# An expert stage on Trainium2: chunk ring of eight, and residual rows added by an accumulating scatter

## The reference, cut to what matters

```python
x = x + _L0_ffn_ref(_L0_cond_ref(x, ...), ...)      # conv, 4-bit weights, two low-rank terms
z = _L1_cond_ref(x, cond_128, ...)                  # per batch entry a 64x64 kernel

logits = zf @ gate_w.T + gate_b                     # 8 experts
selected = argmax(softmax(logits), axis=-1)
out = 0
for j in range(8):
    out += where(selected == j, zf @ expert_w[j].T + expert_b[j], 0)
x = x + out
```

## Time and profile before

| | us |
|---|---|
| median of 3 runs (1543.79 to 1545.86) | 1543.8 |
| the profiled execution: its own time | 1545.5 |
| its span | 1544.0 |
| TensorE busy | 1443.0 (93%) |
| VectorE busy | 1123.6 (73%) |
| ScalarE busy | 762.5 (49%) |
| GpSimd busy | 153.5 (10%) |
| `wlr` (L1019), 184 operations, mean 1219 ns | 212.9 |
| `whr` (L693), 184 operations, mean 1056 ns | 188.0 |
| `add_rows` (L1013), 23 operations, mean 1215 ns | 28.0 |

### The profile page before, as it was taken

How to read it: one execution, slowest core, us unless ns; L and a number is a source line. 1 busy time by engine, 2 the same in 40 slices (tenths; PEclk the granted TensorE clock), 3 DMA queues, 4 the chain that set the end, 5 groups by cost and what they waited for, 6 DMA issues and landing times.

```text
span 1544.0 us, 20802 instructions
## 1 busy us (share of the span) xinstructions
PE 1443.0 (93%) x6831; PEld 1173.4 (76%) x6831; DVE 1123.6 (73%) x1058; ACT 762.5 (49%) x845; POOL 153.5 (10%) x217
## 2 busy tenths in 40 slices
PE   6886899999999999999999999999989599999996
PEld 5676788888888888888888888888855477777774
DVE  3562787877888787788778778784234488888885
ACT  3461554454555445455554544551112166666763
POOL 0112200000000000000000000000011223343440
PEclk8898999999999999999999999999999599999998
DMA  5567565655665565565556546555646655877960
GB/s 161 195 206 275 209 222 221 263 217 192 256 241 199 213 262 217 192 257 221 211 220 261 215 188 264 226 212 189 235 163 231 216 144 141 304 206 235 317 181 6
DMA packets 104366, 331.30 MB, mean 215 GB/s; under 512 B 17361, under 2 KB 24921, under 8 KB 104249
## 3 DMA queue, kind: packets, MB, share of 16 engines
q1 hardware_dynamic: 80478, 258.22, 44.8%
q0 software_dynamic: 22512, 71.32, 15.0%
q10 hardware_dynamic: 1298, 0.68, 0.2%
HBM read 295.04 MB, written 46.14 MB: 221 GB/s over the span
## 4 chain that ended last, share of the span: by engine, by line
PE 84%; DVE 5%; DMA 3%; ACT 3%; issue 2%; ACTq 1%; POOL 0%; SPq 0%; DVEq 0%; POOLq 0%
PE pair L1045 25%; PE pair L1047 24%; PE pair L1046 24%; PE pair L1094 3%; PE pair L1189 2%; DVE wlr L1019 2%; DMA am<-am_dn 1%; PE pair L1246 1%; DMA batch_kernels<-aggs 1%; PE pair L1104 1%; ACT whr L693 1%; PE pair L1196 1%; DVE wf L761 1%; PE pair L1107 1%; PE pair L1204 1%
## 5 line engine op out<-in xcount | busy, mean ns | idle before, releaser
L761 DVE TENSOR_TENSOR wf<-wf,term 128x1024 f32<-128x1024 f32 x308 | 377.1, 1224 | 93.7 <-ACT term L554 74.9
L554 ACT ACTIVATE term<-codes 128x1024 f32<-128x1024 int32 x308 | 321.1, 1055 | 106.9 <-DVE wf L761 106.9
L1045 PE MATMUL pair<-wh,hh 128*128 128x512 f32 x704 | 275.2, 391 | 4.0 <-DVE acc L800 2.6
L1047 PE MATMUL pair<-wh,hl 128*128 128x512 f32 x704 | 274.7, 390 | 0.0
L1046 PE MATMUL pair<-wl,hh 128*128 128x512 f32 x704 | 274.6, 390 | 0.0
L1045 PE MATMUL pair<-ring,wh 128*128 128x512 f32 x656 | 255.5, 390 | 1.3 <-issue 1.3
L800 DVE TENSOR_TENSOR acc<-acc,pair 128x1024 f32<-128x1024 f32 x176 | 214.2, 1217 | 57.8 <-PE pair L1047 57.8
L1047 PE MATMUL pair<-ring,wl 128*128 128x512 f32 x656 | 255.2, 389 | 0.0
L1046 PE MATMUL pair<-ring,wh 128*128 128x512 f32 x656 | 255.2, 389 | 0.0
L1019 DVE TENSOR_TENSOR wlr<-wraw,whr 128x1024 fp32r<-128x1024 f32 x184 | 212.9, 1219 | 3.3 <-ACT whr L693 3.3
L582 ACT ACTIVATE wh<-wf 128x1024 fp32r<-128x1024 f32 x44 | 46.7, 1060 | 339.2 <-DVE wf L776 339.2
(11 more groups left out here) (162 smaller groups left out, 1398.9 us busy)
## 6 DMA issues: line engine op xcount, KB each, us to landing
ring<-x_parts SPq DMA_DIRECT2D x320, 512.0 KB, 7.4
wraw<-exp_w SPq DMA_DIRECT2D x64, 512.0 KB, 10.9
x_parts<-stage POOLq DMA_DIRECT2D x24, 512.0 KB, 8.3
xg<-exp_b POOLq DMA_DIRECT2D x23, 512.0 KB, 7.2
codes<-codes_up SPq DMA_DIRECT2D x22, 512.0 KB, 7.5
codes<-codes_dn SPq DMA_DIRECT2D x22, 512.0 KB, 6.1
am<-am_dn SPq DMA_DIRECT2D x22, 512.0 KB
acc<-x_nat POOLq DMA_DIRECT2D x16, 512.0 KB, 10.3
```

The costliest lines, as they stand in the source:

```text
L554: return nc.scalar.activation(out, codes[:, n % 2], ACT.Relu, scale=scale, bias=-scale * bend)
L761: nc.vector.tensor_tensor(whole(n), whole(n), term[:, e % 2], op).then_inc(term_added, 1)
L1045: mm(ps, ah, bh, start=first, stop=False)
L1047: return mm(ps, al, bh, start=False, stop=last)
```

## The change

The rings `whr` and `wlr` get eight slots, so ScalarE writes chunk kt of a tile once TensorE is done with chunk kt of the tile before. `rows_transposed` moves from after chunk 3 to after chunk 1; `z_high` and `z_low` of a tile now come after chunk 2 of its own conversion. `x_dram` is gone: SP stores the tiles of `acc` straight into `out`. `gather_x` and VectorE's `add_rows` are gone. Instead ScalarE copies a finished tile's sums from PSUM to `yg` (four buffers) in `rows_out`, after all eight chunks of the next tile; GpSimd adds the bias to `yg` by an accumulating DMA; and the scatter is an indirect DMA that adds `yg` to the rows of `out`. `zidx` has four entries, shared by gather and scatter, so a tile's gather now waits for the scatter of four tiles earlier.

```diff
@@ -100,7 +100,6 @@
         bd_dram = nc.dram_tensor("batch_kernels", (B, CH, CH), F32, kind="Internal").ap()
         x1_dram = nc.dram_tensor("x1_parts", (NC, KT, P, 2 * CHUNK), F32, kind="Internal").ap()
         z_dram = nc.dram_tensor("z_rows", (N, L), F32, kind="Internal").ap()
-        x_dram = nc.dram_tensor("x_rows", (N, L), F32, kind="Internal").ap()
 
         ident = sb(ctx, "ident", [P, P])
         ones = sb(ctx, "ones", [P, P])
@@ -184,13 +183,11 @@
         stages = (stage0, stage1, stage2, ring)
 
         moe = ExitStack()
-        whr = sb(moe, "whr", [P, 4, L], F32R)
-        wlr = sb(moe, "wlr", [P, 4, L], F32R)
+        whr = sb(moe, "whr", [P, KT, L], F32R)
+        wlr = sb(moe, "wlr", [P, KT, L], F32R)
         zth = sb(moe, "zth", [P, 2, KT, ST], F32R)
         ztl = sb(moe, "ztl", [P, 2, KT, ST], F32R)
-        xg = sb(moe, "xg", [P, 4, L])
         wraw = sb(moe, "wraw", [P, 2, KT, L])
-        zg = sb(moe, "zg", [P, 2, L])
         tri = sb(moe, "tri", [P, P])
         iota_i = sb(moe, "iota_i", [P, P], I32)
         iota_f = sb(moe, "iota_f", [P, P])
@@ -226,8 +223,9 @@
         loads = sb(moe, "loads", [P, 2, NSP], I32)
 
         through = sb(moe, "through", [P, E], I32)
-        zidx = sb(moe, "zidx", [P, 2], I32)
-        xidx = sb(moe, "xidx", [P, 4], I32)
+        zidx = sb(moe, "zidx", [P, 4], I32)
+        yg = sb(moe, "yg", [P, 4, L])
+        zg = sb(moe, "zg", [P, 2, L])
         moe.close()
 
         pair = [ctx.enter_context(nc.psum_tensor(f"pair{i}", [P, 1024], F32)) for i in range(4)]
@@ -262,10 +260,9 @@
         x_stored = [sem(f"x_stored{i}") for i in range(2)]
         iotas, route_const, route_dve, route_mm, row_ready, slot_mm, table_ready, tiles_ready = (sem(n) for n in (
             "iotas", "route_const", "route_dve", "route_mm", "row_ready", "slot_mm", "table_ready", "tiles_ready"))
-        zidx_ready, xidx_ready = sem("zidx_ready"), sem("xidx_ready")
+        zidx_ready = sem("zidx_ready")
         zg_in = [sem(f"zg_in{i}") for i in range(2)]
-        xg_in = [sem(f"xg_in{i}") for i in range(4)]
-        xb_in = [sem(f"xb_in{i}") for i in range(4)]
+        yb_in = [sem(f"yb_in{i}") for i in range(4)]
 
         wraw_in = [[sem(f"wraw_in{b}{i}") for i in range(KT)] for b in range(2)]
         whr_ready, wlr_ready, chunk_mm = sem("whr_ready"), sem("wlr_ready"), sem("chunk_mm")
@@ -380,7 +377,7 @@
 
             for t in range(TILES):
                 sp.wait_ge(acc_added, TILES * (UNITS - 1) + t + 1)
-                sp.dma_start(x_dram[t * P:(t + 1) * P], acc[:, t]).then_inc(x_stored[t % 2], 16)
+                sp.dma_start(out[t * P:(t + 1) * P], acc[:, t]).then_inc(x_stored[t % 2], 16)
             sp.wait_ge(bdg_zero, 1)
             sp.dma_start(gts[:], gate_t).then_inc(gts_in, 16)
             for i in rounds(sp, TILES // 2):
@@ -467,59 +464,47 @@
                 pool.wait_ge(z_stored[k], 16 * TILES // 2)
                 pool.wait_ge(x_stored[k], 16 * TILES // 2)
 
-            def gather_z(i, s):
-
+            def gather(i, s):
+
+                wait(pool, out_done[s % 4], i * 16 + 16 * (s // 4))
                 wait(pool, tr_mm, i * 4 + s - 1)
                 pool.sem_inc(pool_passed, 1)
-                nc.gpsimd.tensor_copy(zidx[:, s % 2:s % 2 + 1], table[:, bass.ds(i * 4 + s, 1)]).then_inc(zidx_ready, 1)
+                nc.gpsimd.tensor_copy(zidx[:, s % 4:s % 4 + 1], table[:, bass.ds(i * 4 + s, 1)]).then_inc(zidx_ready, 1)
                 wait(pool, zidx_ready, i * 4 + s + 1)
                 pool.sem_inc(pool_passed, 1)
-                pool.indirect_dma_start(zg[:, s % 2], None, z_dram, bass.IndirectOffsetOnAxis(zidx[:, s % 2:s % 2 + 1], 0),
+                pool.indirect_dma_start(zg[:, s % 2], None, z_dram, bass.IndirectOffsetOnAxis(zidx[:, s % 4:s % 4 + 1], 0),
                                         bounds_check=last_row, oob_is_err=False).then_inc(zg_in[s % 2], 16)
-
-            def gather_x(i, s):
-
-                wait(pool, out_done[s % 4], i * 16 + 16 * (s // 4))
-                pool.sem_inc(pool_passed, 1)
-                nc.gpsimd.tensor_copy(xidx[:, s % 4:s % 4 + 1], table[:, bass.ds(i * 4 + s, 1)]).then_inc(xidx_ready, 1)
-                wait(pool, xidx_ready, i * 4 + s + 1)
-                pool.sem_inc(pool_passed, 1)
-                pool.indirect_dma_start(xg[:, s % 4], None, x_dram, bass.IndirectOffsetOnAxis(xidx[:, s % 4:s % 4 + 1], 0),
-                                        bounds_check=last_row, oob_is_err=False).then_inc(xg_in[s % 4], 16)
 
             def add_bias(i, s):
                 e = pool.value_load(eti[0:1, bass.ds(i * 4 + s, 1)], min_val=0, max_val=E - 1)
-                wait(pool, xg_in[s % 4], i * 16 + 16 * (s // 4 + 1))
-                pool.sem_inc(pool_passed, 1)
-                pool.dma_start(xg[:, s % 4], exp_b[bass.ds(e, 1)].broadcast_to([P, L]), accum_op=ALU.add
-                               ).then_inc(xb_in[s % 4], 16)
-
-            def scatter(i, s):
                 wait(pool, y_ready, i * 4 + s + 1)
                 pool.sem_inc(pool_passed, 1)
-                pool.indirect_dma_start(out, bass.IndirectOffsetOnAxis(xidx[:, s % 4:s % 4 + 1], 0), xg[:, s % 4], None,
-                                        bounds_check=last_row, oob_is_err=False).then_inc(out_done[s % 4], 16)
+                pool.dma_start(yg[:, s % 4], exp_b[bass.ds(e, 1)].broadcast_to([P, L]), accum_op=ALU.add
+                               ).then_inc(yb_in[s % 4], 16)
+
+            def scatter(i, s):
+
+                wait(pool, yb_in[s % 4], i * 16 + 16 * (s // 4 + 1))
+                pool.sem_inc(pool_passed, 1)
+                pool.indirect_dma_start(out, bass.IndirectOffsetOnAxis(zidx[:, s % 4:s % 4 + 1], 0), yg[:, s % 4], None,
+                                        bounds_check=last_row, oob_is_err=False, compute_op=ALU.add).then_inc(out_done[s % 4], 16)
 
             def tile(i, s):
                 left = NS if not isinstance(i, int) else NS - 4 * i - s
                 if left > 2:
-                    gather_z(i, s + 2)
-                    add_bias(i, s + 2)
-                scatter(i, s)
-                if left > 3:
-                    gather_x(i, s + 3)
-
-            gather_z(0, 0)
-            gather_z(0, 1)
-            for s in range(3):
-                gather_x(0, s)
-            add_bias(0, 0)
-            add_bias(0, 1)
+                    gather(i, s + 2)
+                add_bias(i, s)
+                if not (isinstance(i, int) and i == s == 0):
+                    scatter(*((i, s - 1) if s else (i - 1, 3)))
+
+            gather(0, 0)
+            gather(0, 1)
             for i in rounds(pool, NS // 4):
                 for s in range(4):
                     tile(i, s)
             for s in range(NS % 4):
                 tile(NS // 4, s)
+            scatter(NS // 4, NS % 4 - 1)
             for k in range(4):
                 pool.wait_ge(out_done[k], 16 * len(range(k, NS, 4)))
 
@@ -689,21 +674,29 @@
                 for kt in range(KT):
                     for b in range(2):
                         act.wait_ge(wraw_in[b][kt], load[b])
-                    wait(act, chunk_mm, i * 32 + KT * s + kt - 3)
-                    nc.scalar.activation(whr[:, kt % 4], wraw[:, bass.ds(buf, 1), kt].rearrange("p a n -> p (a n)"),
+
+                    wait(act, chunk_mm, i * 32 + KT * (s - 1) + kt + 1)
+                    nc.scalar.activation(whr[:, kt], wraw[:, bass.ds(buf, 1), kt].rearrange("p a n -> p (a n)"),
                                          ACT.Copy).then_inc(whr_ready, 1)
-                    if kt == 5 and not (isinstance(i, int) and 4 * i + s == NS - 1):
-                        z_high(i, s + 1)
+                    if kt == 2:
+                        z_high(i, s)
+                if not (isinstance(i, int) and i == s == 0):
+                    rows_out(*((i, s - 1) if s else (i - 1, 3)))
+
+            def rows_out(i, s):
+                act.wait_ge(chunk_mm, i * 32 + KT * (s + 1))
+                wait(act, out_done[s % 4], i * 16 + 16 * (s // 4))
+                nc.scalar.activation(yg[:, s % 4], pair[s % 2][:], ACT.Copy).then_inc(y_ready, 1)
 
             for k in range(2):
                 act.wait_ge(x_stored[k], 16 * TILES // 2)
             act.wait_ge(tiles_ready, TABLES)
-            z_high(0, 0)
             for i in rounds(act, NS // 4):
                 for s in range(4):
                     convert_high(i, s)
             for s in range(NS % 4):
                 convert_high(NS // 4, s)
+            rows_out(NS // 4, NS % 4 - 1)
 
         @block.vector
         def _(dve):
@@ -1007,34 +1000,22 @@
                 nc.vector.tensor_tensor(ztl[:, s % 2], pair[2 + s % 2][:].rearrange("p (k s) -> p k s", k=KT), zth[:, s % 2],
                                         ALU.subtract).then_inc(ztl_ready, 1)
 
-            def add_rows(i, s):
-                wait(dve, chunk_mm, i * 32 + KT * (s + 1))
```

(24 more changed lines are left out.)

## The result

The changed kernel takes 1588.2 us (median of 4 runs, 1584.2 to 1596.5) against 1543.8: ratio 1.029, 95% interval 1.0267 to 1.0312. It is slower by 44 us.

What follows compares the result with a forecast made beforehand. TensorE, busy 93%, was taken as the bound, with GpSimd's ring late next. Terms -3.8 - 3.8 + 25.0 - 2.2 + 4.5 + 4 = +23.7 us on 1543.8 gave 1567 us; own range 1552 to 1586, over rivals 1522 to 1592.

Steps and rivals of the forecast that it cites:

- the third rival: Accumulating scatter pays a full landing of its own: quiet chain 18.3 us, total +53.5, 1597 us; chance 0.12.
- Conversion: Weight chunks on VectorE and ScalarE: eight slots remove 0.95 us per tile, 22 intervals, 20.9 us if nothing else is late.
- The quiet ring: Products through bias, scatter, index copy and gather to transposes, without loads: 16.1 us; ten intervals at 12.7 against 13.08, -3.8.
- the last four: Last four tile intervals, whose gathers fetch nothing as routing fills 20 of 23 tiles: 12.13 us each, -3.8.
- bytes follow in the same queue: Scatter's bytes come after the bias's in one queue: 3.0 us added, bounds 0 (full overlap) and 5.2 (full landing).
- Beside the loads: Chain under weight loads: 25.1 us, two tiles 34.4 (+8.2) in long stretches, 30.5 (+4.3) in short; together +25.0.
- the four pairs: Two-tile rounds in the four weight-load stretches: two at +8.2 us, two at +4.3.
- Clock: TensorE at half rate after long pauses: 1.8 us lost in each of two pairs, +4 with rounding.
- Start: TensorE's first product in the stage: three chunks converted by then, -2.2 us (-1.1 if the clock's rise doesn't move).
- End: Last products to last scatter: copy 1.1, bias 5.2, scatter at about 6.5 instead of 2.0, +4.5 us (bounds +3.5 and +8).
- the chain fits: Rival: transfers overlap, chain stays under 15.0 us also with loads, all 22 intervals at 12.13; -18.6, 1525 us; chance 0.27.
- Its sign: What would prove the scatter's full landing: bias landings in quiet above 7 us in the new profile.

Runs made afterwards that it cites:

- run 1: Changed kernel with two GpSimd calls swapped: scatter of tile s-1 issued before the bias addition of tile s; 1543.4 us, ratio 0.9979.
- run 2: Changed kernel, GpSimd's order kept, scatter given its own copy of the row numbers so the gather waits for no scatter; 1548.4 us, ratio 1.0007.
- run 7: Kernel before with only the rings of eight and the earlier transposes, plus the gather one tile earlier (s+3); 1514.8 us, ratio 0.982.
- run 8: Changed kernel with own scatter index and gather one tile earlier; bias now written plainly two tiles ahead, VectorE adds the sums; 1514.5 us, ratio 0.9791.
- run 3: Changed kernel without the weight transfers of experts 2 to 7, whose tiles use the weights of experts 0 and 1; 1559.2 us, ratio 1.0081.
- run 5: Kernel before with rings of eight chunks and earlier transposes alone; residual gather, bias and plain scatter as before; 1545.8 us, ratio 1.0012.
- run 4: Changed kernel with a scatter that writes instead of adding, so the residual is left out of the result; 1569.6 us, ratio 1.0145.
- run 10: Repeat in five rounds of the kernel before with rings of eight and the gather one tile earlier; 1514.4 us, ratio 0.9817.

## Why the prediction was right, and where its sum was off

The direction and the mechanism held: TensorE waits for gathered rows, held up by the ring from the sums through the bias, the scatter and the index copy to the next gather, and runs 1 and 2 show it. The size did not: +24 us were forecast and +44 measured. 1588 us lies inside the range over all rivals (1522 to 1592), but 2 us above the forecast's own (1552 to 1586), and nearer the third rival's 1597 than the 1567. Its terms:

- **Conversion.** Right in kind, too small. The pause for `wlr` is gone, and an undisturbed tile takes 11.79 us, not 12.13. I had priced a chunk at 1.42 us from four chunks of which the first, behind the pause, takes 1.49 us where the next take 1.36; undisturbed it is (11.79 - 0.8) / 8 = 1.37. The 22 intervals had 28 us to win, not 21: runs 7 and 8 do win 30 us.
- **The quiet ring: a term that was mis-sized.** I had 16.1 us from products to transposes and a small gain from it (-3.8 for ten intervals, -3.8 for the last four). With all pairs quiet, my terms with start and end make about -8 us; run 3 shows +12. In the round shown above, ScalarE's last conversion and copy and the issue take 2.8 us instead of 2.3, the scatter lands 8.0 after its issue (7.0 to 9.5 in the other quiet rounds of this kernel) where 16.1 allowed 6.9, and index copy and wait take 2.0 instead of 1.2, since the copy next to a scatter takes up to 1.2 us where it took 0.3. With 1.3 from the bias's issue to the scatter's and 4.5 for a quiet gather (1268.38 to 1272.89) that is 18.6; two tiles take 18.6 + 0.8 + 6 x 1.37 = 27.6, 13.8 each, against a measured mean of 13.4 in run 3. The scatter's "bytes follow in the same queue" was the wrong model for its price by 1 to 2 us; the bounds (0 and 5.2) did hold it.
- **Beside the loads.** By the sum, loads and clock take 25.0 + 4 us, and 3 more that the four pairs would have gained in quiet: 32. Measured, 1.029 against 1.0081, it is 32 too. That they agree so well is luck, for the parts don't. The sum had two pairs of 34.4 us and two of 30.5. The trace has five, of 34.5, 34.9, 32.8, 36.4 and 33.3 (1300.31 to 1369.68, 1414.36 to 1483.57, 1497.36 to 1530.61): the short loads, too, held up a whole ring. Together they stand 41 us above five pairs of before, 26.2 each; 29 were forecast, and all else, -7.6 in the sum, is +4. The price of a loaded scatter was about right: 11.1 to 13.7 us after its issue in six rounds, against 12.0 in the sum.
- **Clock: the other term that was mis-sized.** +4 forecast, two pauses at 1.8 us lost each. In the profiled execution it is 17 us (the account above). I had gone by one drop in a 5 us idle time and expected a dip only behind the longest waits. Here the clock also fell around waits of 2 and 3 us, some of them in quiet tiles.
- **Start** -2.2 forecast, -2.4 seen. **End** +4.5 forecast, +5.3 seen.
- **Rivals.** That the chain fits is out: transposes wait 14 times. By the Trainium skill, DMA: Bandwidth & Descriptors, on the anatomy of a GpSimd DMA, each 0.5 MB transfer would have landed in an estimated 3.2 us; the bias here took 4.9 at least, 6.6 at the median and 11.0 at most, and the accumulating scatter 7.0 and more in the rounds in which the index copy waited for it. The trace does not agree with that figure. That the scatter pays a full landing of its own was nearer in its quiet price (18.3 us for the ring, measured 18.6) than my forecast's 16.1, and its 1597 us nearer the measured 1588. Its sign, bias landings above 7 us in quiet, isn't what happened: in run 3 their median is 5.3 and the longest 7.3. That its time is near owes much to the clock and the fifth pair, which it did not have either.

The sum did count when TensorE wants the rows (one tile and two chunks after the products). What I never asked, and what runs 1, 2 and 5 fell short by, is whether that lead is enough without the ring: the change's own gain shortens it. Moving the transposes from chunk 3 to chunk 1 and shortening the tile from 13.1 to 11.8 us took 4 us from it, and beside a load one gather alone needed 11.3 (run 2).

## What to carry to other kernels

A wait in an engine's program order is paid by all that stands behind it on that engine. Before a buffer's release is tied to a later transfer, follow the ring round once and compare its length with its period; here one swap of two calls was worth 3% of the whole kernel. And when a change makes the engine in front faster, lengthen the lead of what feeds it: the same ring of eight is worth nothing with the gather two tiles ahead, and 30 us with it three ahead.

## What the runs showed of the hardware

- The granted clock fell to its lower level around waits of TensorE as short as 2 us. In the changed kernel a wait of 1.97 us ends at 1286.85, one tile after one of 3.05 behind which the clock stayed at 1.00. Busy time by stretch behind the wait of 1.97 us:

```profile
1288.00:1292.00 4.00, 4.00 (x12) 3.12 (x11) 0.99 (x2) 1.72 (x2) 0.83 (x1) 0.57 1.04 174
1292.00:1296.00 4.00, 4.00 (x20) 3.27 (x19) 3.98 (x4) 3.23 (x4) 1.15 (x2) 1.00 0.16 31
```

Four microseconds of uninterrupted matmuls at a granted 0.57 hold 12 of them instead of 20. The length of a wait alone doesn't tell: in run 3 the 13.6 us behind a wait of 1.94 us have 0.87, and the 12 us behind waits of 1.93 and 2.12 us have 1.00. The kernel before paused 0.8 us in every tile and kept 1.00.
- Issuing an indirect scatter cost GpSimd more when it accumulates (1993 ns at the mean for the accumulating scatter, 1349 for the plain one of run 4), and beside weight loads single issues took up to 5.8 us (run 5).
- An accumulating indirect scatter of 0.5 MB landed about 2 us later than a plain one in quiet tiles (7.0 to 9.5 us against 4.8 to 7.0).
- The longest time to landing of a 512 KB weight chunk varies between executions of one kernel: 16.6 and 23.9 us (runs 7 and 10).
